# Graph and expert layers on one core: the completion signals of TensorE move from matmuls to drains

## What is computed

```python
edge_index = jnp.stack([src, dst])            # 106250 edges, sorted by dst
x = x + _L0_gnn_ref(_layernorm(x), edge_index, edge_weight, ...)   # two weighted graph layers, relu, a projection
x = x + _L0_ffn_ref(_layernorm(x)[None], ...)                      # 2 of 8 experts for all rows, 256 -> 512 -> 256
x = x + _L1_gnn_ref(_layernorm(x), edge_index, ...)                # two graph layers normed by degree
x = x + _L1_ffn_ref(_layernorm(x)[None], ...)                      # 8 experts with a capacity, 256 -> 1024 -> 256

def _gcn_layer(x, W, b, src, dst, norm, n_nodes):
    xt = x @ W
    msg = xt[src] * norm[:, None]
    return relu(segment_sum(msg, dst, num_segments=n_nodes) + b)
```

## Time and profile before

| | us |
|---|---|
| runs (2) | 5611.9 and 5638.83, median 5625.36 |
| span of the profiled execution | 5647.3 |
| layer 0, about 418 to 1603 us of the span | 1185 |
| layer 1, about 1603 to 2962 | 1359 |
| first experts, about 2962 to 3355 | 393 |
| layer 2, about 3355 to 4215 | 860 |
| layer 3, about 4215 to 5075 | 860 |
| second experts, from about 5075 | 572 |
| busy: TensorE / VectorE / GpSimd | 4017.9 / 3072.1 / 2967.7 |

### The profile page before, as it was taken

The page is one execution under the profiler, slowest core; times in us unless marked ns, Lnnn a source line. Parts: engine busy times, 40 slices in busy tenths (PEclk is TensorE's granted clock), DMA queues, the critical chain, the costliest instruction groups (busy, mean ns, idle before and its releaser), DMA issues.

```text
span 5647.3 us, 64923 instructions
## 1 busy us (share of the span) xinstructions
PE 4017.9 (71%) x21108; PEld 3177.4 (56%) x21109; DVE 3072.1 (54%) x7978; ACT 1485.5 (26%) x4028; POOL 2967.7 (53%) x3232
## 2 busy tenths in 40 slices
PE   7764555555546676777778977788776778785999
PEld 6653433334335466666666755666655666664766
DVE  7765645555447655555555565555546554443434
ACT  6502322232232222222223322222231111124221
POOL 7736466666656555555640016555556555543233
PEclk9987777776678777777779988899988998997999
DMA  2423433333333222222221013333333332225231
GB/s 89 122 68 93 118 96 97 96 96 96 97 89 87 78 80 79 80 80 80 82 67 34 20 60 87 89 92 90 90 102 97 102 93 84 83 77 176 69 104 54
DMA packets 272106, 489.99 MB, mean 87 GB/s; under 512 B 85684, under 2 KB 176805, under 8 KB 271635
## 3 DMA queue, kind: packets, MB, share of 16 engines
q0 software_dynamic: 139312, 377.94, 23.8%
q1 hardware_dynamic: 125336, 101.03, 5.9%
q10 hardware_dynamic: 7118, 6.83, 0.4%
HBM read 426.41 MB, written 62.17 MB: 87 GB/s over the span
## 4 chain that ended last, share of the span: by engine, by line
PE 39%; another core or an unknown queue 23%; DVE 22%; issue 10%; ACT 3%; DVEq 2%; POOL 1%; DMA 1%; ACTq 0%; SPq 0%; POOLq 0%
PE PSA L1020 11%; PE PSA L1164 5%; DVE ACC L2016 4%; PE PSA L1411 4%; PE PSA L1397 4%; PE PSA L1173 3%; PE PSA L1298 3%; PE PSA L1314 3%; DVE XIN L1989 2%; DVE XT L1989 2%; PE PSA L985 1%; PE PSA L979 1%; DVE WORK L2282 1%; PE PSA L1149 1%
## 5 line engine op out<-in xcount | busy, mean ns | idle before, releaser
L853 POOL DMA_INDIRECT WORK<-tab,SRC x2632 | 2522.8, 958 | 2146.8 <-issue 768.0
L2016 DVE TENSOR_TENSOR ACC<-ACC,PSA 64x256 f32 x1360 | 568.9, 418 | 1457.7 <-remote 959.4
L1020 PE MATMUL PSA<-WORK,XIN 128*128 128x256 f32 x3192 | 960.0, 454 | 458.0 <-ACT XIN L1491 341.5
L1020 PEld LDWEIGHTS PSA<-WORK,XIN 128*128 128x128 f32 x3192 | 711.0, 233 | 612.1 <-issue 492.5
L1020 PE MATMUL PSA<-WORK,XT 128*128 128x256 f32 x2072 | 594.5, 437 | 161.4 <-ACT XT L1491 85.4
L1020 PEld LDWEIGHTS PSA<-WORK,XT 128*128 128x128 f32 x2072 | 439.4, 222 | 248.9 <-issue 172.6
L1149 PE MATMUL PSA<-WORK 128*128 128x256 bf16 x784 | 161.6, 290 | 327.4 <-DVE WORK L2282 98.2
L1173 PE MATMUL PSA<-WORK,XT 128*128 128x42 f32 x832 | 153.8, 350 | 211.8 <-DVE WORK L1989 211.7
L1149 PEld LDWEIGHTS PSA<-WORK 128*128 128x128 bf16 x784 | 69.4, 104 | 379.8 <-issue 230.4
L1989 DVE TENSOR_TENSOR XIN<-PSA,DST 128x512 f32<-128x512 f32 x412 | 279.1, 679 | 2.5 <-DVE PSA L2323 1.4
L1173 PEld LDWEIGHTS PSA<-WORK,XT 128*128 128x128 f32 x832 | 145.8, 260 | 223.7 <-DVE WORK L1989 221.7
(11 more groups left out here) (492 smaller groups left out, 6899.0 us busy)
## 6 DMA issues: line engine op xcount, KB each, us to landing
WORK<-tab,SRC POOLq DMA_INDIRECT x2632
ACC<-in_L_ffn_w SPq DMA_DIRECT2D x16, 1024.0 KB
tab<-WORK SPq DMA_DIRECT2D x98, 128.0 KB
slots_x<-FILL SPq DMA_DIRECT2D x4, 2080.0 KB
ACC<-slots_x SPq DMA_DIRECT2D x8, 910.0 KB
tab<-ACC SPq DMA_DIRECT2D x49, 128.0 KB
WORK<-tab SPq DMA_DIRECT2D x49, 128.0 KB
before_y<-X SPq DMA_DIRECT2D x7, 896.0 KB
```

The lines of the kernel that those rows point to most:

```text
L853: po.indirect_dma_start(out=rows[:, 0:width], out_offset=None, in_=tab[:, :], in_offset=bass.IndirectOffsetOnAxis(ap=SRC[:, c:c + 1].bitca ...
L1020: last = pe.matmul(PS[h][:, 0:D], chosen[:, j * P:(j + 1) * P], rows[:, 0:D], start=(j == 0), stop=(j == Q - 1))
L2016: return ve.tensor_tensor(rows, rows, PS[h][half, 0:D], ALU.add)
```

## The change

The signals of all those pieces are taken off the last matmul. A drain (`pe.drain()`), an instruction of its own in TensorE's queue, is put behind each piece and carries the signal. The matmuls, their order, all waits and all other engines stay as they are. Counted from the loops, there are 306 such signals in layer 0 (208 products, 49 turns, 49 tile products), 601 in layer 1 (208 products, 147 turns and tile products, 2 + 36 counts, 208 moves), 622 in layer 2 (132 products, 98 turns and tile products, 196 counts and 196 sums of units), 627 in layer 3 (132 products, 392 of units, 103 turns and gate products), and one behind (`turn_ends`): 2157 drains. The signals of the degree sums before layer 0 and of both dense blocks stay on matmuls.

```diff
--- before.py
+++ after.py
@@ -1030,7 +1030,7 @@
                     rows = X[:, n * D + c * P:n * D + (c + 1) * P] if n < NT else \
                         WG[:, (n - NT) * DG + c * P:(n - NT) * DG + (c + 1) * P]
                     last = pe.transpose(slot_n(n)[:, c * P:(c + 1) * P], rows, IDN[:, :])
-                last.then_inc(s_lt, 1)
+                pe.drain().then_inc(s_lt, 1)
 
             def gate_node(n):
                 if n < NT + KC:
@@ -1038,7 +1038,7 @@
                 for c in range(KC):
                     last = pe.matmul(slot_g(n), XG[n % 2][:, c * P:(c + 1) * P] if n < NT + KC else ONE[:, :],
                                      GWS[:, c * EM:(c + 1) * EM], start=(c == 0), stop=(c == KC - 1))
-                last.then_inc(s_gate, 1)
+                pe.drain().then_inc(s_gate, 1)
 
             def gate_steps(g):
                 for k in gates_of(g):
@@ -1056,7 +1056,7 @@
                     pe.wait_ge(s_ut, t + 1)
                 for c in range(KC):
                     last = pe.transpose(early_f(t)[:, c * P:(c + 1) * P], sums(t)[:, c * P:(c + 1) * P], IDN[:, :])
-                last.then_inc(s_tt, 1)
+                pe.drain().then_inc(s_tt, 1)
 
             def tile_product(layer, into, turned_rows):
                 if not layer:
@@ -1073,7 +1073,8 @@
                         pe.wait_ge(s_a5, t)
                     else:
                         pe.wait_ge(s_put, NT * TAB2 + t)
-                tile_product(layer, early_p(t), early_ft(layer, t)).then_inc(s_u5 if layer else s_u2, 1)
+                tile_product(layer, early_p(t), early_ft(layer, t))
+                pe.drain().then_inc(s_u5 if layer else s_u2, 1)
 
             def up_third(into, turned_rows):
                 for fo in range(KC):
@@ -1092,13 +1093,15 @@
                 pe.wait_ge(s_ft, NT + t + 1)
                 if 0 < t <= TAIL:
                     pe.wait_ge(s_h7, t)
-                up_third(early_p(t), FT1[t % 2]).then_inc(s_u3, 1)
+                up_third(early_p(t), FT1[t % 2])
+                pe.drain().then_inc(s_u3, 1)
 
             def early_down(t):
                 pe.wait_ge(s_h7, t + 1)
                 if 0 < t < TAIL:
                     pe.wait_ge(s_a3, t)
-                down_third(early_d(t), H7T[t % 2]).then_inc(s_d3, 1)
+                down_third(early_d(t), H7T[t % 2])
+                pe.drain().then_inc(s_d3, 1)
 
             def redo_third():
                 with pe.Fori(0, NT):
@@ -1130,13 +1133,13 @@
                 for k in range(2):
                     last = pe.matmul(counts_part(k), ONE[0:1, :], TILE[0:1, (2 * n + k) * NK:(2 * n + k + 1) * NK],
                                      start=True, stop=True)
-                last.then_inc(s_ks, 1)
+                pe.drain().then_inc(s_ks, 1)
 
             def count_kept(n):
                 pe.wait_ge(s_kc, 3 + n + 1)
                 for k, ones in enumerate((ONE, TRI)):
                     last = pe.matmul(counts_part(k), ones[:, :], FLAG[n % 2], start=True, stop=True)
-                last.then_inc(s_ks, 1)
+                pe.drain().then_inc(s_ks, 1)
 
             def count_unit(layer, n):
 
@@ -1148,7 +1151,7 @@
                 for j in range(2):
                     last = pe.matmul(UNP[:, j * D:(j + 1) * D], low[:, j * P:(j + 1) * P], units[:, j * D:(j + 1) * D],
                                      start=True, stop=True)
-                last.then_inc(s_ub, 1)
+                pe.drain().then_inc(s_ub, 1)
 
             def sum_unit(layer, n):
 
@@ -1164,7 +1167,7 @@
                         last = pe.matmul(UNS[i][t % 2], UNC[i][n % 3][:, h * P:(h + 1) * P], part_of(4 * u + h, c),
                                          start=(u == 0 and h == 0 and c == 0),
                                          stop=(u == NUN - 1 and h == 3 and c == C3 - 1))
-                last.then_inc(s_ud, 1)
+                pe.drain().then_inc(s_ud, 1)
 
             def move_kept(k):
                 pe.wait_ge(s_kc, NUMBERED + 2 + k + 2)
@@ -1194,7 +1197,8 @@
                         pe.wait_ge(s_free, 4 + BEGIN[1] + g - 2)
                     if layer >= 2 and g >= 2:
                         pe.wait_ge(s_free, 4 + BEGIN[layer] + g - 1)
-                    product(SEL[g % NS], rows_of(layer, g), bank_of(layer, g)).then_inc(s_p, 1)
+                    product(SEL[g % NS], rows_of(layer, g), bank_of(layer, g))
+                    pe.drain().then_inc(s_p, 1)
                     if layer == 3:
                         gate_steps(g)
                     if g in early:
```

## The result

The changed kernel takes 6200.8 us (median of 2 runs, 6191.8 to 6209.8) against 5625.4: a ratio of 1.103, with an interval of 1.095 to 1.110. I had forecast 5250, so the sign is wrong.

What follows compares the result with a forecast made beforehand. It took late matmul signals during gathers as the brake: gathers pace layer 0, TensorE and VectorE layer 1, nearly TensorE layers 2 and 3. -100 -190 -45 -45 = -380 on 5647.3 gives 5267, less 22 for earlier runs, said as 5250; range 5080 to 5960.

Steps and rivals of the forecast that it cites:

- Signals in time: All layers: drain signals do not come late as matmul signals do; 100 us less in layer 0, gains in later layers.
- the hold: Interval in which signals of finished matmuls are held back while gathers run; 4.87 us per 29.6 us round in layer 0.
- remote: Profile's name for waits on an unknown releaser, 959.4 us at VectorE's add; their vanishing was a sign of being right.
- the stops of GpSimd in layer 0: Sign of being right: layer 0's gathers would run without GpSimd's 4.87 us stops.
- The drains on TensorE: Each drain costs TensorE 0.3 us where work would have followed at once, 647 us together (345 to 970).
- What lies on the path: Drains hide behind gathers in layer 0; layer 1 gains 190 us, layers 2 and 3 45 us each.
- The first rival: Drain waits out late signals and TensorE stands still with it, all layers: about 1060 us more, 6690; chance 0.18.
- The second rival: Drain's signal is as late as a matmul's, nothing else changes; drains in layers 1 to 3 cost 280 us, 5905; chance 0.10.
- the payback: Late signals go, but drains at 0.45 us cost layers 2 and 3 60 us each; sum -40, 5585 us; chance 0.10.
- Two rules against the rows: Skill's signalling rule would make the change cost some part of 647 us; its weight-load rule gave 231 us for 2157 drains.

Runs made afterwards that it cites:

- bare drains: Kernel before, signals left on matmuls, a drain without a signal added behind each of 2157 pieces: 5191.6 us, ratio 1.100; again 5189.4 us, ratio 1.097.

## Why the prediction was wrong

**"Signals in time" (-100 in layer 0, and the gain in all layers): this step failed.** What I read in the trace before holds: signals of matmuls came late while gathers ran, and without gathers they don't (603 and 588 us in layers 2 and 3 instead of 834 and 830). It does not follow that a drain escapes. The drain's own signal is prompt, but the drain ends only when the hold does: VectorE and TensorE go on together at 871.43 and 871.49. The sum, each a difference between two sessions: late signals cost the kernel before 5623.2 - 4730.3 = 893 us (888 on the one chip that showed both), and the changed kernel 6192.8 - 5185.2 = 1008. None of it came back. I gave the trace's silence ("no drain stands in it") the answer that I wanted; with no row for it, the rule of the Trainium skill that I quoted should have weighed more than a hope that another path exists. My sign for it was badly chosen besides: waits for "remote" vanish at a drain whether or not it is late. Of the signs that could tell, the stops of GpSimd in layer 0 did not go (its waits there for VectorE's release, DVEq, are 366.8 us and were 264.5), and the clock, which was to pass 0.75 in both first layers, fell to 0.70 from 0.73 in layer 0 and rose to 0.77 from 0.75 in layer 1.

The room that I saw was mis-sized as well. I had layer 0's floor at 208 groups x 5.0 = 1040 us and so at most 145 us to gain; GpSimd has only 768 instructions in that stretch of 1185 us, which at 1.25 us a gather is 960 us, and without late signals the layer takes 958.

**"The drains on TensorE" (0.3 us each, 647 us): mis-sized by a fifth.** The parts were right: the tail of the last matmul, first weights in the open, something for the drain. Measured are 0.37 us in layers 2 and 3, 0.36 to 0.42 for products, 0.35 in the dense stretch; the 0.05 for the drain itself, for which I had no row, is 0.03 by the second drain. 2157 x 0.37 = 798 us of TensorE's time.

**"What lies on the path": layer 0 right as far as its price goes, the rest not.** In layer 0 the 306 drains do hide behind the gathers (958 us either way without late signals); its +101 come only with late signals. In layer 1 I had 190 us less; the drains alone make it 116 more. In layers 2 and 3 I had TensorE at 851 us and counted on the clock for the rest. The clock did rise (0.93 and 0.92 from 0.90 and 0.89), but 851 was to stand against 860 only because the holds were taken as gone. Without them the kernel before needs 660, the gathers' floor, and the drains make 835 and 811 of it. There the total of 5185 lies below my 5250: not for my reasons, since the kernel before is at 4730.

**The first rival happened, the drain that waits out the hold with TensorE standing still** (chance 0.18, 6690 us). Its mechanism is in the trace (6.31 and 13.70 us of standing, no remote waits). Its size was too large by 490 us: I had charged 504 us for the holds (127 + 127 + 190 + 60); what they added is 1008 - 893 = 115. It also put them in the wrong place: by layer the change lost 105, 85, 195 and 187 us with late signals and 0, 116, 175 and 153 without, so nearly all that they add lies in layer 0, for which I had 60, and layer 1, for which I had 190, even lost less. Most of the standing seems to be time in which TensorE would have waited anyway. Layer 0 bears this out: TensorE is idle there for 1185 - 628 = 557 us before and 1286 - 684 = 602 after. For the other layers it is argued and not measured. Its 555 us for the drains of layers 1 to 3 are 455 measured.

**The second rival** (the drain's signal as late, TensorE going on; 5905) is refuted by the same rows, since TensorE does not go on, **the payback** (5585) by the absence of any gain.

**Two rules against the rows.** The Trainium skill ("PSUM — Partial Sum Buffer", section "Engine vs sequencer instructions") says to signal from the producing matmul and that a drain waits for an idle engine. I had set the late signal against its first half. The traces agree with the second half: TensorE starts nothing until the drain is through, and that wait is what costs. For the first half, the changed kernel and bare drains take the same time without late signals (5185.2 and 5189.4 us), so there the drain's signal is no sooner. With late signals no run sets the two beside each other; that the drain gave nothing back is read from the 1008 against the 893 us.

## What to carry to other kernels

A drain on TensorE is paid at about 0.37 us where more work would have followed at once, and at nothing where TensorE has room under another engine's floor; count the drains and look at which layers still have room before moving signals to them. Beside late signals it costs more (680 product drains: 0 us without them, 156 with). When a signal comes late, ask what event it reports: a drain, which waited for the same event here, was as late, and stalled the engine besides. Before explaining a trace by something odd in it, take the same kernel in a second session: here the oddity came and went, with a sixth of the time.

## What the runs showed of the hardware

- Signals of matmuls can come ten microseconds late while GpSimd issues indirect gathers (a product that ends at 836.42 us by the profile reaches VectorE at 846.47; a drain in the same place came 13.6 us late, 821.12 to 834.75). The same program on the same chip shows this in one session and not in another (5618 and 4730 us). In the trace before, every such wait of over 14 us in all is for a signal of TensorE.
- Plain transfers that GpSimd issues, at 122 to 128 GB/s, hold no signal in the session in which the gathers do.
- A drain costs TensorE 0.35 to 0.42 us where work would have followed at once (210 drains 74.4 us, 1249 drains 461 us, 132 drains 56 and 48 us), and a second drain right behind the first 0.03 us more (70 us for 2157, one run).
